# One query product for two heads, maxima of two heads on separate row halves of TensorE, and one reduction for both

## The reference, cut to what matters

```python
q = (x @ Wq + bq).reshape(B, S, H, DK)      # H = 16 heads, DK = 64
k = x @ Wk + bk                             # one key head, DK = 64
v = x @ Wv + bv
scores = jnp.einsum('bshd,btd->bhst', q, k) / np.sqrt(DK)
w = jax.nn.softmax(scores, axis=-1)
out = jnp.einsum('bhst,btd->bshd', w, v).reshape(B, S, H * DV)
return out @ Wo + bo
```

## Time and profile before

| what | value |
|---|---|
| median of three runs | 1417.2 us (1414.25 to 1417.55) |
| the profiled execution | 1409.84 us |
| its span, first to last instruction | 1408.0 us |
| mean granted TensorE clock in it | 0.962 |
| busy: PE, PEld, DVE, ACT, POOL | 1286.0, 760.0, 1011.7, 708.6, 270.9 us |

### The profile page before, as it was taken

How to read it: one execution, slowest core, us unless ns; L and a number is a source line. 1 busy time by engine, 2 the same in 40 slices (tenths; PEclk the granted TensorE clock), 3 DMA queues, 4 the chain that set the end, 5 groups by cost and what they waited for, 6 DMA issues and landing times.

```text
span 1408.0 us, 22235 instructions
## 1 busy us (share of the span) xinstructions
PE 1286.0 (91%) x7377; PEld 760.0 (54%) x7377; DVE 1011.7 (72%) x2393; ACT 708.6 (50%) x1300; POOL 270.9 (19%) x314
## 2 busy tenths in 40 slices
PE   4569988999989998999899999999999979999997
PEld 2335435554545555555454555555655538686844
DVE  7776866578857875787668766876687747677875
ACT  3126544544464445444554445544545448677741
POOL 3033222200120012001200120012000205454630
PEclk9569998999999999999999999999999989999999
DMA  2051433000210021003000200020000246465451
GB/s 75 0 158 61 151 108 138 29 17 19 84 32 17 18 85 32 18 18 85 31 17 19 85 32 17 18 85 32 18 17 19 62 136 207 155 214 170 144 179 48
DMA packets 69299, 100.25 MB, mean 71 GB/s; under 512 B 29196, under 2 KB 45132, under 8 KB 65220
## 3 DMA queue, kind: packets, MB, share of 16 engines
q1 hardware_dynamic: 54628, 66.23, 15.2%
q0 software_dynamic: 11344, 31.64, 6.9%
q10 hardware_dynamic: 3216, 0.97, 0.3%
HBM read 59.86 MB, written 38.68 MB: 70 GB/s over the span
## 4 chain that ended last, share of the span: by engine, by line
PE 73%; DVE 16%; issue 3%; DMA 2%; ACT 2%; SPq 2%; POOL 1%; DVEq 0%; ACTq 0%; POOLq 0%
PE bank L1420 14%; PE bank L1392 8%; PE bank L1348 7%; PE bank L1431 6%; PE bank L1393 6%; PE bank L1256 5%; PE bank L1258 5%; PE bank L1257 5%; PE bank L1452 4%; DVE mneg L987 3%; PE bank L1272 2%; PE bank L1262 2%; DVE q_lm L981 2%; PE bank L1307 2%; PE bank L1289 1%
## 5 line engine op out<-in xcount | busy, mean ns | idle before, releaser
L815 ACT ACTIVATE wide<-bank 128x512 f32<-128x512 f32 x512 | 301.5, 604 | 493.3 <-PE bank L1393 483.0
L987 DVE TENSOR_REDUCE mneg<-bank 128x1 f32<-128x512 f32 x512 | 347.2, 685 | 182.2 <-PE bank L1348 176.5
L1420 PE MATMUL bank<-wide,v_w 128*32 128x512 f32 x2048 | 249.5, 605 | 0.5 <-issue 0.5
L1348 PE MATMUL bank<-k_hl,q_hh 128*128 128x512 f32 x512 | 208.0, 407 | 34.9 <-DVE mneg L987 21.7
L1392 PE MATMUL bank<-q_hh,k_hl 128*128 128x512 f32 x512 | 234.7, 458 | 1.7 <-ACT wide L815 1.4
L1393 PE MATMUL bank<-q_lm,k_h 65*128 65x512 f32 x512 | 203.6, 398 | 0.0
L1392 PEld LDWEIGHTS bank<-q_hh,k_hl 128*128 128x128 f32 x512 | 97.0, 189 | 131.1 <-issue 89.5
L614 POOL TENSOR_TENSOR rs<-rs,power 128x4 f32<-128x4 f32 x24 | 24.6, 1026 | 626.4 <-DVE rs L889 626.4
L1348 PEld LDWEIGHTS bank<-k_hl,q_hh 128*128 128x128 f32 x512 | 98.1, 192 | 72.6 <-issue 51.7
L1431 PE MATMUL bank<-wide,ones 128*32 128x512 f32 x992 | 129.1, 592 | 0.0
L684 POOL DMA_INDIRECT y_rows<-y_m,to_u x92 | 104.2, 1132 | 127.0 <-DVE y_m L1114 105.1
(11 more groups left out here) (231 smaller groups left out, 1970.4 us busy)
## 6 DMA issues: line engine op xcount, KB each, us to landing
w_t<-w_rows SPq DMA_DIRECT2D x23, 1024.0 KB
x_rows<-part_h POOLq DMA_DIRECT2D x65, 258.0 KB, 6.1
inv<-inverse_scratch SPq DMA_DIRECT2D x124, 128.0 KB, 2.9
w_rows<-w_t SPq DMA_DIRECT2D x8, 1024.0 KB, 4.9
x_m<-x_rows SPq DMA_DIRECT2D x23, 258.0 KB, 3.6
stage<-in_L_ffn_W SPq DMA_DIRECT2D x16, 256.0 KB, 5.2
yab<-y_rows POOLq DMA_DIRECT2D x8, 512.0 KB, 9.4
xin<-in_L_attn_x SPq DMA_DIRECT2D x8, 256.0 KB, 5.9
```

Of the source, the lines that this page charges most:

```text
L815: act.activation(wide[:, st.g % WIDE, :], ps, ACT.Exp, scale=SCALE1).then_inc(wide_full, 1)
L987: dve.tensor_reduce(mneg[:, (gh // 2) % 2, col:col + 1], ps[:], X, ALU.max, negate=True)\
L1348: into(("mx", gh, j), lambda ps: pe.matmul(ps[:], q_hh[:, gh % HEADS, P * j:P * j + P], k_hl[:, n % 2, :], start=True, stop=True))
L1420: pe.matmul(ps_out[0][rows, :], v_w[:, n, c, TILE * d:TILE * d + TILE], weights, start=(c == 0), stop=(c == TT - 1))
```

## The change

- A query product serves two heads. `wq_h` and `wq_l` hold each head once, and 128 output columns are two heads: head 2p on rows 0 to 63, head 2p + 1 on rows 64 to 127. One product (three matmuls) at s = 2 takes the place of two at s = 1 and s = 5.
- `round_q` rounds each half with an instruction of its own (64 rows), two in a row at s = 2, and `lo_q` follows at s = 3, two in a row, ahead of VectorE's layer 0 work.
- The other row half of `q_hh` is no longer computed: SyncE copies it by two DMAs per pair (`copy_queries`), each after the rounding of its head, and `first` waits for them (`q_copied`) before the pair's first step.
- The scores for the maxima of the two heads are two matmuls of 64 rows: head 2p with `k_h1` on rows 0 to 63, head 2p + 1 with a new copy of the rounded keys `k_hh` on rows 64 to 127. They go to two neighbouring small banks, at s = 0, 2, 4, 6 only. The part that the rounding left of the keys no longer enters the maxima.
- `maximum` takes both banks in one instruction (128 x 2 x 512).
- `Ring` skips a bank, where needed, so that the pair of banks is 0 and 1 or 2 and 3, and counts their release once. The order within s = 2 is maxima first, then the query product.
- `WO_AT` moves from k = 17 to k = 18 of the next row, layer 0's slot 10 from k = 2 to k = 1.

```diff
+            first = name[0] == "mx" and name[1] % 2 == 0
+            if first:
+                n += n % 2
...
-        ahead_ = gh + LEAD + s // TT
-        if 0 <= ahead_ < H * NB:
-            events.append(("mx", ahead_, s % TT))
-        if s == TT + 1 and 0 <= gh + 2 < H * NB:
-            events.append(("mt", (gh + 2) // 2))
-        if s % TT == 1 and 0 <= ahead_ + 1 < H * NB:
-            events.append(("q", ahead_ + 1))
+        here, total = gh // 2, H // 2 * NB
+        if s == TT + 1 and 0 <= here + 1 < total:
+            events.append(("mt", here + 1))
+        if s % 2 == 0:
+            pair, j = (here + 1, s // 2 + 2) if s < TT else (here + 2, s // 2 - 2)
+            if 0 <= pair < total:
+                events.append(("mx", pair, j))
+        if s == QUERY_AT and 0 <= here + 2 < total:
+            events.append(("q", here + 2))
...
+            def copy_queries(pair):
+
+                for b in range(2):
+                    gh = 2 * pair + b
+                    here, there = slice(DK * b, DK * b + DK), slice(DK - DK * b, P - DK * b)
+                    sp.wait_ge(qh_done, gh + 1)
+                    sp.dma_start(q_hh[there, gh % HEADS, :].bitcast(F32), q_hh[here, gh % HEADS, :].bitcast(F32))\
+                      .then_inc(q_copied[pair % 2], 16)
...
-            def round_q(gh):
-                ps, _ = filled(act, ("q", gh))
-                if gh >= HEADS:
-                    act.wait_ge(first_full, last_step(gh - HEADS) + 1)
-                act.activation(q_hh[:, gh % HEADS, :], ps[:], ACT.Identity, bias=bq[:, gh % H:gh % H + 1])\
-                   .then_inc(qh_done, 1)
+            def round_q(pair):
+                ps, _ = filled(act, ("q", pair))
+                for b in range(2):
+                    gh, rows = 2 * pair + b, slice(DK * b, DK * b + DK)
+                    if gh >= HEADS:
+                        act.wait_ge(first_full, last_step(gh - HEADS) + 1)
+                    act.activation(q_hh[rows, gh % HEADS, :], ps[rows, :], ACT.Identity, bias=bq[rows, gh % H:gh % H + 1])\
+                       .then_inc(qh_done, 1)
...
-            def maximum(gh, j):
-                ps, free = full(("mx", gh, j))
-                col = TT * (gh % 2) + j
-                dve.tensor_reduce(mneg[:, (gh // 2) % 2, col:col + 1], ps[:], X, ALU.max, negate=True)\
+            def maximum(pair, j):
+                i, _ = ring.at(("mx", 2 * pair, j))
+                full(("mx", 2 * pair, j))
+                _, free = full(("mx", 2 * pair + 1, j))
+                dve.tensor_reduce(mneg[:, pair % 2, j:2 * TT:TT], small[:, i:i + 2, :], X, ALU.max, negate=True)\
                    .then_inc(free, 1)
...
+            def scores_for_maximum(pair, j):
+
+                n = 2 * pair // H
+                if 2 * pair % H == 0 and j == 0:
                     read_out(pe, ("k", n))
-                pe.wait_ge(qh_done, gh + 1)
-                into(("mx", gh, j), lambda ps: pe.matmul(ps[:], q_hh[:, gh % HEADS, P * j:P * j + P], k_hl[:, n % 2, :],
-                                                         start=True, stop=True))
+                pe.wait_ge(qh_done, 2 * pair + 2)
+                for b, keys in enumerate((k_h1, k_hh)):
+                    gh, rows = 2 * pair + b, slice(DK * b, DK * b + DK)
+                    into(("mx", gh, j), lambda ps: pe.matmul(ps[:], q_hh[rows, gh % HEADS, P * j:P * j + P],
+                                                             keys[rows, n % 2, :], start=True, stop=True))
```

More of the change, by code:

```diff
@@ L42, in __init__, with freed, before @@
     def __init__(self, banks, order):
-        self.total, self.place = [0] * banks, {}
-        for n, name in enumerate(order):
+        self.fills, self.frees, self.last = [0] * banks, [0] * banks, [None] * banks
+        self.place, self.free, self.prior, n = {}, {}, {}, 0
+        for name in order:
             assert name not in self.place, name
-            self.place[name] = (n % banks, self.total[n % banks])
-            self.total[n % banks] += 1
+            first = name[0] == "mx" and name[1] % 2 == 0
+            if first:
+                n += n % 2
+            i = n % banks
+            self.place[name], self.prior[name] = (i, self.fills[i]), self.last[i]
+            self.fills[i] += 1
+            self.last[i] = name
+            if first:
+                self.free[name] = (i + 1, self.frees[i + 1] + 1)
+            else:
+                self.frees[i] += 1
+                self.free[name] = (i, self.frees[i])
+            n += 1
     def at(self, name):
         return self.place[name]
+    def freed(self, name):
+        return self.free[name]
+    def before(self, name):
+        return self.prior[name]
 class Links:
@@ L397, in two_layers @@
         m_loaded = [sem(f"m_loaded{i}") for i in range(2)]
+        q_copied = [sem(f"q_copied{i}") for i in range(2)]
         sums_stored, sums_loaded = [sem(f"sums_stored{i}") for i in range(2)], sem("sums_loaded")
@@ L802, in _ @@
                         src = raw[:, n, :].rearrange("p (h d) -> p h d", d=DK)
-                        for hi in copies(wq_h[:, 8 * n:8 * n + 8]):
-                            last = act.activation(hi, src, ACT.Identity)
-                        last.then_inc(split_h, 1)
+                        act.activation(wq_h[:, 8 * n:8 * n + 8], src, ACT.Identity).then_inc(split_h, 1)
             act.wait_ge(split_l, 2)
@@ L1207, in _ @@
             for st in steps:
+                if split_pair(st) is not None:
+                    lo_q(split_pair(st))
                 if st.kind in ("pre", "o"):
@@ L1211, in _ @@
                             next(cuts[n], None)
-                if split_head(st) is not None:
-                    lo_q(split_head(st))
                 for event in head_events(st):
```

93 lines of the change are left out of this document (51 added, 42 removed).

## The result

The changed kernel takes 1455.1 us (median of four runs, 1452.1 to 1456.2) against 1415.7 for the kernel before in the same session: a ratio of 1.028, with an interval of 1.025 to 1.030. It is 39 us slower, where 13 us faster were forecast, and it lies outside the range. The profiled execution spans 1452.9 us, 44.9 more than before.

The account below looks back on a forecast made before the run. The prediction took the rows to be bound by TensorE; per row -3.6 + 3.9 - 2.0 = -1.7 us, over some 7.6 rows -13 us, so 1417.2 - 13 = 1404 us. The range was 1350 to 1440 us.

Parts of the forecast that it names:

- halves B: Half blocks of steps s = 2 to 5: two roundings delay an exponential, bare ones 1.04 us longer; 3.9 us lost per row.
- the term for VectorE: Merged reductions, `lo_q` ahead of layer 0 and longer half blocks cut TensorE's waits for VectorE: 2 us per row back.
- halves A: Half blocks of steps s = 6, 7, 0, 1: 0.45 us gained each, eight times per row, 3.6 us.
- The price of a couple: Two heads' maxima matmuls on row halves: 0.64 us with overlap and tiling change against 0.47, a loss of 0.17.
- The rival with no price of the change: Row tiles overlap without a tiling-change cost, two maxima matmuls taking 0.24 us: -9.3 us per row, 1347 us; chance 0.22.
- the two without overlap: Row tiles not side by side: undrained 0.47 us, 1392 us, chance 0.10; drained 0.88 us, 1455 us, chance 0.13.
- covered: Half blocks s = 2 to 5 whose other work hides the delay: pairs 2, 6, 7 unchanged; pairs 0 and 5 partly.
- The rival with VectorE as the bound: `lo_q`'s 0.9 us lost in the four dense pairs: +3.6 us per row over the forecast, 1431 us; chance 0.10.
- `lo_q`'s wait: At s = 3 `lo_q` waits for the second rounding with layer 0 work queued behind it: up to 0.9 us idle.
- One row times 7.6: Whole run: -1.7 us per row over seven rows and six pairs of the last, some 7.6 rows: -13 us.
- The edits at nothing: Query copies, bank pairs, `k_hh` and weight splitting were forecast to cost nothing; weight splitting at most 3 us gained.

Follow-up runs that it names:

- full_array: Changed kernel with both maxima matmuls of a couple on the whole array, using another operand (result not the reference's): 1432.0 us, 1.011 of the kernel before.
- s1_first_full_array: Changed kernel with query product at s = 1, VectorE taking k = 32's maxima first, maxima matmuls on the whole array (not the reference's result): 1370.4 us, 0.970.
- query_s1: Changed kernel with the query product one step earlier, at s = 1 instead of s = 2: 1409.7 us, 0.995 of the kernel before.
- max_first_k32: Changed kernel with VectorE taking the maxima of k = 32 ahead of its layer 0 work: 1438.6 us, 1.015 of the kernel before.
- query_s1_max_first: Changed kernel with the query product at s = 1 and the maxima of k = 32 ahead of VectorE's layer 0 work: 1389.5 us, 0.984 of the kernel before.
- one_rounding: Changed kernel with one query rounding of 128 rows into its own tile and four copies per pair instead of two: 1424.2 us, 1.008 of the kernel before.

## Why the prediction was wrong, point by point

In the forecast's own sum, per row and for rows 2 to 4, 5.0 us are off: -1.7 was forecast and +3.3 came. The steps that failed are the term for halves B (+3.9, measured +5.9), the term for VectorE (-2.0, measured -0.3 with what the clock moved) and the term for halves A (-3.6, measured -2.3). Beyond that the five other rows lost 23 us more than these, for which there was no term.

**The price of a couple: right.** Overlap of the row tiles (3 ns apart), 0.09 in, an exposed load behind it, next full-array matmul after 0.75 instead of 0.77; half A bare 6.03 against 6.06; the couple 0.14 dearer than two full-array matmuls, forecast 0.17. The Trainium skill, page TensorEngine Tiling (Array Packing), section Key Properties, has the rule that a change of tiling mode drains TensorE. The trace agrees for row tiles as it did for column tiles (0.09 in, the next full-array matmul 0.43 after the couple). The same page, section Theoretical Speedup, has a gain of up to 2x for a contraction of 64. Of that the trace shows that the two matmuls start together; with the change of tiling the couple is dearer than two full-array matmuls (1.08 against 0.94 us). `full_array` (-23) and `s1_first_full_array` (-19) show what it is worth in this kernel. The rival with no price of the change fell, and so did the two without overlap.

**Half B: the mechanism right, the term too small.** The roundings at s = 2 do stand before the exponential of s = 3, TensorE holds the couple of s = 4 to 3.52 (forecast 3.5), and `first` of s = 5 waits. But a rounding of 64 rows was taken at 0.59, as if it were one of 128, and takes 0.71, so that `first` of s = 5 starts 4.64 after the half block instead of 4.48. From there to the value block it is 0.78 where the forecast left 0.68 (its text names only 0.57 of that): the transpose and the change into column tiles take 0.20, not 0.12. Together 8.13 instead of 7.87, +1.3 instead of +1.04 each. Pair 6 was called covered by the gates' products and loses 0.9. Pairs 0 and 5 lose 0.53 and 0.54 (1.07, forecast 0.8). Pair 2 is covered, as forecast. In all 5.9 for pairs 0 to 6, forecast 3.9.

In pair 7, at k = 58, row 3 gets 2.2 of it back, but there the kernel before was in a stretch at lower clock and the changed one was not (rows 0, 1 and 6 don't have this): its six layer 0 matmuls take 3.92 us at a granted clock of 0.57 (675.90 to 679.80), and 2.25 in the changed kernel. The other 0.6 is waiting for VectorE, 0.51 + 1.36 before and this now:

```profile
697.85 2.81 PE L1318 MATMUL small<-x0t,w 128*128 128x512 f32 x6 [1.29 <-DVE mneg L1033]
```

The two rows of windows, before and after:

```profile
671.68:687.86 16.18, 14.30 (x67) 7.27 (x63) 11.00 (x33) 8.60 (x13) 3.32 (x4) 0.89 0.13 42
```

```profile
693.60:707.59 13.99, 12.70 (x67) 6.16 (x63) 11.26 (x32) 9.21 (x14) 2.06 (x3) 1.00 0.21 63
```

Over rows 1 to 6 TensorE's waits for ScalarE rose from 3.5 to 38.4 us, 5.8 per row. `query_s1` (-45 us) moves this term: it is the largest that an experiment moved, and of its 5.9 us per row the forecast had counted 3.9.

**Half A: too large.** The 0.45 of a bare half was multiplied by eight. Those at k = 38, 54 and 62 and the one beside the projection come near it (0.4 to 0.5); the ones at k = 6, 22 and 46 gain 0.06, 0.14 and 0.31, together 2.3 instead of 3.6, and the eighth, k = 30, loses.

**VectorE: its gain did not come, and at k = 30 it was a loss.** The forecast took 2.0 us per row back from TensorE's waits for VectorE. In row 3 those at k = 58 and 59 fell by 0.6 and the one in the half block from k = 30 rose by 0.8, so that nothing came back; over the whole run they are 84.7 instead of 91.4 us, 6.7 less where 15 less were forecast. The half block at k = 30 lost 1.9: 0.8 by the longer wait and 1.5 by the lower clock behind it, less some 0.4 gained as in other halves A. In rows 2 to 4 each kernel has one stretch at 1.2 GHz per row: before the change it stood at k = 59, now it stands at k = 32, so some 1.5 of the 1.9 lost there and of the 2.2 regained at k = 58 are one loss that moved. I had looked at the bank ring in bare pairs only ("in a bare pair the couples of s = 4 and 6 take the banks of s = 2 and 4") and not at the steps where layer 0's transposes draw from the same ring in the step in which the couple does. With couples, two banks are taken and given back at once, behind whatever VectorE has queued. `max_first_k32` shows what wait and lower clock at that place cost together: -17 us. The rival with VectorE as the bound is not this: VectorE has idle time in row 3 (102.95 busy of 146.88), and it was late by its order. `lo_q`'s wait, that rival's price, did not decide: TensorE's waits that `lo_q` ended fell from 26.1 us to 6.7 over the run.

**One row times 7.6: wrong.** Worked out from half blocks, row 3 is -2.3 (halves A) + 1.9 (k = 30) + 5.9 (halves B) - 2.2 (k = 58) = +3.3. Rows 2 to 4 are like it. Eight such rows would be 27 us, not 50. Rows 1 and 6 lose 5 us more than that: 3 at k = 58, where the relief is missing, and 1.7 at k = 34. Half blocks from k = 34 of rows 3 and 6 with their granted clock:

```profile
643.32:651.45 8.13, 6.98 (x44) 2.98 (x41) 6.28 (x9) 4.61 (x9) 0.00 (x0) 1.00 0.18 38
...
1086.42:1096.23 9.81, 8.66 (x44) 3.33 (x40) 7.17 (x10) 4.61 (x9) 0.00 (x0) 0.83 0.15 31
```

The same work takes 1.7 us more in row 6, and all of that is the value block at the lower clock (granted 0.52 from 1091.82 to 1095.20):

```profile
1089.95 0.50 PE L1397 MATMUL small<-k_h,q_hh 64*128 64x512 f32 x1 [0.54 <-ACT q_hh L793]
...
1091.06 0.50 PE L1443 MATMUL bank<-q_hh,k_hl 128*128 128x512 f32 x1 [0.61 <-ACT wide L857]
...
1091.82 3.61 PE L1471 MATMUL bank<-wide,v_w 128*32 128x512 f32 x16
```

Before it stand the two waits of a bare half B, and before those the wait at k = 30. Over the run the mean granted clock is 0.951 against 0.962. Between the levels of 2.4 and 1.2 GHz that is 2 x 0.049 x 1452.9 = 142 us at the lower one, against 107 before. The value block takes 3.61 at the lower level and 1.92 at the upper, so of 35 us more at most half, some 17, is lost time; the forecast had no term for that. No run changes the clock alone; in the stretches shown, the lower clock stands behind waits and makes them dearer. `query_s1_max_first`, at 0.959 over 1387.6 us, is back at some 114 us. The clock does not set the time alone: `query_s1` is at 0.952, some 135 us, and is faster than the kernel before.

**The edits at nothing.** No wait for `q_copied` appears anywhere, as forecast, and the copies land in 2.3 us, where 2.9 was taken. The start gained 5.0 us, where at most 3 were allowed. The last row lost 7.9, and its waits say where: TensorE's rose from 20.8 to 28.7 us in it, those for ScalarE by 5.2, for VectorE by 2.0 and for DMAs by 0.7. In row 0, which lost 9.9, they rose by 5.1 (for ScalarE by 6.3, while those for VectorE fell), and its granted clock is 0.92 against 0.96: by the estimate above some 14 us more at the lower level, of which at most 7 are lost. A wait for `q_lm`'s transport shows in the last row of some kernels, in `query_s1` for instance:

```profile
1357.82 0.77 PE L1443 MATMUL bank<-q_hh,k_hl 128*128 128x512 f32 x1 [2.17 <-DMA q_lm<-mrow]
```

In the changed kernel such waits are 1.4 us over the run and 0.5 in the last row, so they are not what it lost.

In sum, per row: forecast -3.6 + 3.9 - 2.0; measured in rows 2 to 4 -2.3 + 5.9 - 0.3 (+1.9 at k = 30, -2.2 at k = 58), and 4.6 more on average in the other rows, 23 us in all. Of these the clock and the missing relief at k = 58 are shown for rows 1 and 6, waits and clock for row 0 and waits for the last row. Row 5 has 1.7 of its 2.1 at k = 30, where behind the same wait of 2.10 the value block takes 3.64 instead of 2.61 (granted clock 0.50). Which edit made the waits of row 0 and of the last row is open.

## What to carry to other kernels

A product may be moved to where TensorE has room, but its reader's engine must have room too: put it so that the rounding falls into the stretch in which ScalarE waits, and look whether an exponential on which TensorE depends stands behind it. Row tiles let two short contractions run side by side and cost a change of tiling with exposed loads; for one couple between full-array matmuls that is a loss of some 0.14 us. Whether several couples in a row would pay is not tested here. When a result takes two banks of a small ring instead of one, look at every step in which something else draws from the ring, not at the plain steps alone, and let the reader go ahead of queued work there, but only where its data is there already (k = 32 gave 17 us, k = 30 as well took 24).

## What the runs showed of the hardware that I had not expected

- A ScalarE instruction on 64 rows is not cheaper than one on 128: it was followed after 0.71 us, in 126 of 128 records, the one of 128 rows of the same 512 elements (`one_rounding`) after 0.59, in 58 of 64. Why the half is dearer is open.
- The two matmuls of a row-tiled couple start 3 ns apart, each 0.49 long, and the array takes the next full-array matmul 0.43 after them.
- A reduction over two banks (128 x 1024) is 1.22 us and is followed after 1.14 (636.89 to 638.03), against the 1.28 of two of 512.
- In kernels whose TensorE is busy 88% of the span and more, single value blocks ran at 1.2 GHz: 16 matmuls took 3.39 us behind a wait of 2.10 (`query_s1`, granted clock 0.53), and 3.61 behind waits of 0.54 and 0.61 (changed kernel, row 6, 0.52), where they take 1.92. The same two waits in row 3 had no fall behind them.
